# A perceiver block on one core: operands moved to one address phase, retention in halves of 64 tokens, cross-attention scores by head in sixteen tiles of the array

## What is computed

```python
x = x + cross_attention(layernorm(x), ctx, ctx)      # x: 32 items x 32 tokens x 512; ctx: 32 x 257 x 512
#   16 heads of 32: scores = Q K^T / sqrt(32); scores <= thr -> -1e9; softmax; @ V; @ Wo.T + bo
x = x + retention_stack(layernorm(x))                # 2 layers
#   xn = LN(x); q, k rotated; scores = (q k^T) * decay, causal inside an item; out = scores v
#   8 heads of 64; y = groupnorm(out); x = (silu(xn Wg) * y) Wo + x
#   x = gelu(LN(x) W1) W2 + x                         # 512 -> 2048 -> 512
x = x + mixture(layernorm(x))                        # 8 experts 512 -> 1024 -> 512, top 2 of each token
```

## Time and profile before

| | |
|---|---|
| median of 3 runs | 1723.44 us (1722.08 to 1725.44) |
| the profiled execution: its time, its span | 1722.73 us, 1720.9 us |
| mean granted TensorE clock | 0.987 |
| cross-attention, keys of item 0 to the last scores | 43 to 547 us |
| retention, layer 0 and layer 1 | 576 to 721 us, 916 to 1062 us |
| feed-forward, layer 0 and layer 1 | 721 to 911 us, 1062 to 1254 us |
| mixture groups | 1290 to 1710 us |

### The profile page before, as it was taken

The page is one execution under the profiler, slowest core; times in us unless marked ns, Lnnn a source line. Parts: engine busy times, 40 slices in busy tenths (PEclk is TensorE's granted clock), DMA queues, the critical chain, the costliest instruction groups (busy, mean ns, idle before and its releaser), DMA issues.

```text
span 1720.9 us, 29176 instructions
## 1 busy us (share of the span) xinstructions
PE 1649.3 (96%) x10832; PEld 1402.7 (82%) x10832; DVE 1087.0 (63%) x2138; ACT 851.2 (49%) x1195; POOL 471.8 (27%) x357
## 2 busy tenths in 40 slices
PE   7999999999998899999998999999989999999997
PEld 6888889889887688788887887887877888888886
DVE  6554454554556767653337676635457989999995
ACT  4444444344444333344335233534416787878873
POOL 1443443444343344300004443300021121211311
PEclk9999999999999899999999999999999999999999
DMA  5011101110111300023224001224342443626612
GB/s 195 26 38 39 37 24 37 37 37 24 61 49 48 113 1 1 25 86 98 91 93 142 1 1 35 88 88 146 133 163 71 172 159 93 246 74 244 215 48 67
DMA packets 35977, 144.00 MB, mean 84 GB/s; under 512 B 4992, under 2 KB 5504, under 8 KB 28672
## 3 DMA queue, kind: packets, MB, share of 16 engines
q1 hardware_dynamic: 30736, 130.98, 21.7%
q0 software_dynamic: 5168, 12.06, 3.5%
HBM read 222.72 MB, written 12.85 MB: 137 GB/s over the span
## 4 chain that ended last, share of the span: by engine, by line
PE 56%; DVE 6%; DMA 2%; issue 1%; ACT 1%; SPq 0%; POOL 0%; DVEq 0%; POOLq 0%; ACTq 0%
PE bank L88 35%; PE bank L1608 9%; PE bank L2083 7%; PE bank L1505 2%; PE bank L2089 2%; PE bank L1592 1%; DVE e_w L2010 1%; DVE rc L1253 1%; DVE rs L1253 1%; DMA A<-xh_d,token 1%; DMA out<-acc_d 0%; PE bank L1517 0%; PE bank L1627 0%; DVE r_xh L1230 0%; DVE r_wg L1239 0%
## 5 line engine op out<-in xcount | busy, mean ns | idle before, releaser
L2010 DVE TENSOR_TENSOR e_w<-e_raw,e_w 128x2048 fp32r<-128x2048 f32 x134 | 302.4, 2284 | 20.3 <-ACT e_w L1892 19.8
L1892 ACT ACTIVATE e_w<-e_raw 128x2048 fp32r<-128x2048 f32 x134 | 256.6, 1918 | 38.4 <-PE bank L2083 19.2
L88 PE MATMUL bank<-e_w,e_xT 128*128 128x512 f32 x1104 | 272.1, 396 | 0.0
L88 PEld LDWEIGHTS bank<-e_w,e_xT 128*128 128x128 f32 x1104 | 204.3, 188 | 42.5
L88 PE MATMUL bank<-wv,ctx 128*128 128x512 f32 x768 | 190.8, 397 | 6.9 <-DVE kT L669 6.9
L88 PE MATMUL bank<-ctx,wk 128*128 128x258 f32 x1536 | 193.3, 285 | 2.1 <-issue 2.1
L88 PE MATMUL bank<-x2T,fw 128*128 128x512 f32 x768 | 190.4, 398 | 4.7 <-DVE fw L1314 4.7
L88 PEld LDWEIGHTS bank<-ctx,wk 128*128 128x128 f32 x1536 | 186.9, 190 | 4.0 <-issue 2.9
L1608 PE MATMUL bank<-fw,hh 128*128 128x512 f32 x768 | 186.1, 391 | 2.7 <-DVE hh L1432 2.7
L88 PEld LDWEIGHTS bank<-x2T,fw 128*128 128x128 f32 x768 | 145.2, 191 | 35.9 <-issue 5.0
L1608 PEld LDWEIGHTS bank<-fw,hh 128*128 128x128 f32 x768 | 143.9, 188 | 34.6 <-issue 2.2
(11 more groups left out here) (253 smaller groups left out, 2674.4 us busy)
## 6 DMA issues: line engine op xcount, KB each, us to landing
e_raw<-in_we SPq DMA_DIRECT2D x138, 1024.0 KB, 5.6
fraw<-in_wf SPq DMA_DIRECT2D x64, 512.0 KB, 3.5
ctxraw<-in_ctx SPq DMA_DIRECT2D x32, 514.0 KB, 3.5
wraw<-in_wa SPq DMA_DIRECT2D x20, 512.0 KB, 4.4
X<-in_x SPq DMA_DIRECT2D x4, 512.0 KB, 7.0
acc_d<-X SPq DMA_DIRECT2D x8, 256.0 KB, 4.5
xh_d<-A SPq DMA_DIRECT2D x8, 256.0 KB, 3.7
out<-acc_d SPq DMA_DIRECT2D x4, 512.0 KB, 5.9
```

The costliest lines, as they stand in the source:

```text
L88: last = nc.tensor.matmul(out, lhs(t, a), rhs(t, b), start=start and n == 0, stop=n == len(steps) - 1)
L1892: nc.scalar.activation(w[pos][:, 0, :, :], raw[pos][:, :, :], ACT.Copy).then_inc(m["w_hi"], 1)
L2010: nc.vector.tensor_tensor(w[pos][:, 1, :, :], raw[pos][:, :, :], r(w[pos][:, 0, :, :]), ALU.subtract).then_inc(m["w_lo"], 1)
```

## The change

- **Addresses.** A helper `to_line` fills up to the next address that is 64 bytes past a multiple of 512; `X`, the identity, `A`, `wk`, `wv`, `wo`, `oT_hl`, `ctx` and with them `e_hT`, `yT` and `x2T0` start there. A row of `ctx` is 384 elements apart (258 used).
- **Scores by head.** `kT` and the queries are plain float32. POOL copies the 32 queries of an item (`qb`) instead of building `qbd`; PE does 16 float32 matmuls of 32x32 with 257 columns, one to each place of the array (head g of a group in rows 32g, group c in columns 32c), into banks 4, 5, 2, 3. The low parts of q and k (L548, L669 on DVE) are gone. `u`, `pr` and `pT` are indexed by g instead of c; the spread matmul has `plast` stationary and the identity moving.
- **Order in cross-attention.** Values of rows 0 to 127, then all scores, then values of rows 128 to 255; `project` (k = 1) and `turn(b-1)` behind them. `attend` is now of item b-2 and stands between the second and the third chunk of the keys. On DVE `heads(b-2)`, `bias_heads` and `project_lo` come before the thresholds, all four thresholds together, then the terms, `last_token(b-1)`, the products. `add_x` moves from k = 1 to k = 2.
- **Retention in halves.** Scores: two 64x64 matmuls per head, for tokens 0 to 63 and 64 to 127 against themselves, in four tiles of the array. `pf` and `decay` are half as wide. `apply_scores`: two matmuls per head over 64 rows.
- `norm_apply` of the next tile stands before the second `rotate`.

```diff
+def to_line(nc, holder, name):
+    gap = (LINE_AT + -nc.sbuf_base // 32 * 32) % LINE      # LINE, LINE_AT = 512, 64
+    if gap:
+        holder(name, [P, gap // 4])
...
-                    def score(b, cs, begin):
...
-                            products(nc, bank[2 + c % 2][:, 0:SKE], range(1), lambda _, h: qbd[:, h, c, :],
-                                     lambda _, h: kT[:, h, c, :]).then_inc(s_ps, 1)
+                    def score():
+                        for g in range(HPC):
+                            rows = slice(g * XD, (g + 1) * XD)
+                            for c in range(DC):
+                                last = nc.tensor.matmul(bank[S_BANK[g]][c * S:(c + 1) * S, 0:SK], qb[rows, c, :], kT[rows, c, :], start=True, stop=True)
+                        last.then_inc(s_ps, 1)
...
+                                if dc == 1 and not (first and k < 2):
+                                    if not (first and k == 2):
+                                        pe.wait_ge(oT_ok, b - 2)
+                                    attend((k - 2) % BPT, b - 2, it if k == 2 and not first else None)
...
-            last = nc.tensor.matmul(bank[7][:, h * E:(h + 1) * E], pf[:, h % 2, h // 2, :], vv[:, h * E:(h + 1) * E], ...)
+            for two in PAIR:
+                last = nc.tensor.matmul(bank[7][two, h * E:(h + 1) * E], pf[two, h % 2, h // 2, :], vv[two, h * E:(h + 1) * E], ...)
...
-                    last_mm = nc.tensor.matmul(bank[2 + i][:, c * P:(c + 1) * P], kT[rows, c, :], qT[rows, c, :], ...)
+                    for two in PAIR:
+                        last_mm = nc.tensor.matmul(bank[2 + i][two, c * E:(c + 1) * E], kT[rows, c, two], qT[rows, c, two], ...)
...
+                            if not (begin or end):
+                                norm_apply(n + 1, t + 1)
                             rotate(n, 1)
```

More of the change, by code:

```diff
@@ L33 @@
 SKE = SK + 1
+CTX_ROW = 3 * P
 XH = 16
@@ L666, in body @@
                             final = last and k == BPT - 1
-                            for dc in range(DC):
-                                dve.wait_ge(k_hi, DC * b + dc + 1)
-                                nc.vector.scalar_tensor_tensor(kT[:, 1, dc, :], bank[K_BANK[dc]][:, 0:SKE], col("bk", dc), r(kT[:, 0, dc, :]),
-                                                               ALU.add, ALU.subtract).then_inc(k_lo, 1)
-                                if dc == 1 and k == 1 and not first:
-                                    project_lo(it - 1)
+                            if k == 2 and not first:
+                                add_x(it - 1)
+                            if not (first and k < 2):
+                                heads((k - 2) % BPT, b - 2)
                             if k == 1 and not first:
-                                add_x(it - 1)
+                                bias_heads(it - 1)
+                                project_lo(it - 1)
                             if final:
@@ L776, in turn @@
                         pe.wait_ge(plast_ok, b + 1)
-                        nc.tensor.matmul(bank[6][:, 0:P], same_head[:, :], plast[:, :, :].rearrange("p c n -> p (c n)"),
+                        if not (isinstance(b, int) and b == 0):
+                            pe.wait_ge(olast_ok, b)
+                        nc.tensor.matmul(bank[6][:, 0:P], plast[:, :, :].rearrange("p g n -> p (g n)"), ident[:, :],
                                          start=True, stop=True).then_inc(spread_ps, 1)
@@ L815, in body @@
                             pe.wait_ge(ctx_lo, b + 1)
+                            if first and k < 2:
+                                pe.wait_ge(zeroed, k + 1)
                             for dc in range(DC):
@@ L829, in body @@
                             if not begin:
-                                pe.wait_ge(k_lo, DC * b + DC)
                                 turn(b - 1)
-                            score(b, (0, 1), begin)
-                            value(1)
-                            score(b, (2, 3), begin)
-                            if not begin:
-                                if not (first and k == 1):
-                                    pe.wait_ge(oT_ok, b - 1)
-                                attend(k - 1, b - 1, it if k == 1 and not first else None)
                     body(0, True)
@@ L1336, in body @@
                                 dve.wait_ge(m["a0_ok"], NT)
-                            if not (begin or end):
-                                norm_apply(n + 1, t + 1)
                             if begin:
@@ L1516, in apply_scores @@
                         for h in range(H):
-                            last = nc.tensor.matmul(bank[7][:, h * E:(h + 1) * E], pf[:, h % 2, h // 2, :], vv[:, h * E:(h + 1) * E],
-                                                    start=True, stop=True)
+                            for two in PAIR:
+                                last = nc.tensor.matmul(bank[7][two, h * E:(h + 1) * E], pf[two, h % 2, h // 2, :], vv[two, h * E:(h + 1) * E],
+                                                        start=True, stop=True)
                         last.then_inc(m["o_ps"], 1)
```

209 lines of the change are left out of this document (106 added, 103 removed).

## The result

| | before | after |
|---|---|---|
| median of the runs, us | 1723.95 (1722.08 to 1725.44, 4 runs) | 1670.92 (1667.59 to 1674.09, 4 runs) |
| profiled execution, us | 1722.73, span 1720.9 | 1671.40, span 1669.6 |
| PE busy, us | 1649.3 | 1602.9 |

The ratio is 0.9693, 95% interval 0.9671 to 0.9714: 53 us faster. The forecast was 1670, between 1654 and 1694.

The account below looks back on a forecast made before the run. PE's queue of matmuls was taken to bound the kernel (96% busy). Gains of 21 + 14.4 + 18.4 - 1 + 1 = 54 us from 1722.7 gave 1669 profiled, about 1670 us median; range 1656 to 1684, 1654 to 1694 with the first two rivals.

Parts of the forecast that it names:

- Addresses: Operands of PE's matmuls moved to 64 bytes past a multiple of 512: 21 us gained (12 to 23).
- the keys' 7.7 us: Key products of cross-attention: 5 ns a matmul gained from the new places, 0.24 us an item, 7.7 us.
- if the keys stay at 120 ns a matmul: Sign in the profile after: key matmuls of 258 columns unchanged at 120 ns would show the forecast wrong.
- Feed-forward: First halves, 32 `up` and 32 `down` runs of 12 matmuls: 0.05 us each from the new places, 3.2 us.
- Mixture: 46 `e_hT` runs and as many behind them: 0.11 us each pair from the new places, 5.1 us.
- Values: 64 value runs of cross-attention: from 2.78 to 2.73 us each by the new places, 3.2 us.
- The first rival: The new places bring nothing elsewhere; 21 us less gained, 1691 us, chance 0.13.
- Scores: Cross-attention: 16 tiled float32 matmuls at 1.0 us replace 1.45 us an item, 14.4 us gained.
- The third rival: Score matmuls' sixteen places don't run together: two at a time 1750 us, chance 0.05; four 1724, chance 0.03.
- Retention: Halves and earlier `norm_apply`: apply 13.6 us, scores 4.8 us, together 18.4 us gained (3 to 24).
- Waits: Cross-attention on PE: waits for kT and `add_x` go, a 1.4 us wait in seven tiles comes; 1 us lost.
- The end of cross-attention: PE's 5.6 us stand for the last normalisation shortens because its softmax starts earlier; 1 us gained.

Follow-up runs that it names:

- keys_width: Changed kernel with the second and fourth key product of each item widened from 258 to 384 and 320 columns; 1695.81 us.
- addr_old: Changed kernel with operand places as before the change (but wo at 192, oT_hl at 96), the rest as changed; 1678.95 us, ratio 0.9742.

## Why the prediction was right

The time came within 1 us of the forecast, and the main mechanisms held; the terms did not all.

1. **Addresses: 21 forecast, 10 measured.** The step that failed is the keys' 7.7 us. I scaled 227 ns for 512 columns to 114 for 258 and took the rest of the 120 for something that the place could cure. keys_width shows a fixed 13 ns in each matmul, and addr_old gives 1.6 us. The prediction called itself wrong "if the keys stay at 120 ns a matmul", and they did: on that count it was wrong, and the sum held because other terms were better. The other terms, start to start, with the places put back against as changed:
   - Feed-forward: 2 us of 3.2 in its runs. The stages gained 3.6, but one layout's executions differ by as much there (201.0 to 203.3 and 140.7 to 142.4 us).
   - Mixture: 2.9 of 5.1. The `e_hT` runs behind an `e_xT` run gained their 0.08 (2.80 to 2.72), and the 44 `e_xT` runs behind `e_hT` their 0.03 (2.754 to 2.725). I had priced all 46 `e_hT` runs like the first kind; about half stand behind a transpose and gained 0.03. The 46 `e_xT` runs behind a transpose lost 0.6 us in all, and why isn't known.
   - Values: 2.1 of 3.2 (185.0 to 182.9 us for 64 runs). `yT` 0.7 and `oT_hl` 0.8, together 1.5 of 1.9.

   The first rival (worth nothing elsewhere) falls with addr_old.

2. **Scores: 14.4 forecast, 32 x (1.45 - 0.85) = 19.2.** The mechanism was right: sixteen places run together. The group took 0.65 us where 0.6 of stream and 0.13 of tail were forecast, and the slower steps beside it 0.2 where some 0.3 of switching was left. How much of the 0.65 is stream isn't shown, so the split of the forecast's 1.0 is untested. The third rival (two or four at a time) is refuted by 0.65 us against its 2.7 or more.

3. **Retention: 18.4 forecast, 18.5 less 0.7 of `yT`.** The total is right, its parts only partly: apply 1.08 for 1.2, scores 0.63 for 0.8, and the neighbours took 0.1 back. I priced the moved `norm_apply` at the 0.2 us wait it removes. Undone alone it costs 10.1 us, not 3.2: once apply is 1 us shorter, PE comes that much earlier to the same wait.

4. **Waits: -1 forecast.** kT's 6.9 went, 8.0 came (7 of 1.2, forecast 1.4; its own terms, 4.2 - 2.9, give 1.3, and PE comes to `attend` at 3.1). The "about 2 more at `attend` for `add_x`" was misread: the 2.1 us were the gaps in front of the keys at the turn of the loop. They went too, so the sum is +1. Not forecast: the lower clock behind the 2.41 us wait, 1.6 us. One trace of the kernel before shows it, so how often it comes is open.

5. **The end of cross-attention: 1 forecast.** PE's idle time there went from 5.6 + 2.0 (for `xn`) to 2.56 + 1.05 + 1.97 us:
```profile
525.61 1.08 PE L790 MATMUL bank<-pT,v 128*32 128x32 f32 x64 [2.56 <-issue]
527.74 1.97 PE L772 MATMUL bank<-ident,pr 128*128 128x128 f32 x8 [1.05 <-POOL pr L362]
...
533.97 3.02 PE L99 MATMUL bank<-r_wq,xn 128*128 128x512 f32 x12 [1.97 <-DVE xn L713]
```
2 us gained.

Together: 54 forecast; -11 addresses, +5 scores, +2 waits, +1.6 the clock in the first item, +1 end, -0.6 retention, -3.4 the start by chance. That is 49 of the 51.3 of the two spans. Of the rest 1.5 lie in the feed-forward stages and 1.2 between `r_wq` and the first `r_xh`, where executions of the new kernels differ by as much (15.4 to 16.7). The closeness is in part luck: errors that cancelled, 11 us of addresses against 5 of scores, 2 of waits and what the clock gave and took.

## What to carry to other kernels

Before a run is scaled from one width to another, fit its pace from two widths: here a full 128 x 128 matmul is its columns and a fixed part, and nothing tried here shortened the fixed part. When the work ahead of a short wait is made shorter, price the edit that removes the wait together with it: the wait grows as work ahead of it is saved, and the two edits were worth 0.5 and 0.4 us a tile apart but 1.4 together. Before a stage's difference is put down to the change, look for stretches of lower clock in both traces. After such a change read the new wait's chain on the other engine for idle stretches; the 8 us that were left went with one instruction moved into one.

## What the runs showed of the hardware

- The pace of full 128 x 128 products depends on how the stationary and the moving operand lie to each other, counted past a multiple of 512 bytes: for 512 columns 227 ns at a difference of 0 (both at 64, or both at 96), about 230 at 320 (`x2T`), 233 to 235 at 64, 96 and 128. With 258 columns it was 1 ns. The Trainium skill, "SBUF — State Buffer", "SBUF: two separate sides", gives PE two independent read ports, one for each operand; these rows disagree in so far as the places interact.
- A run with both operands at the same place pays too when it stands between displaced ones: `fw,hh` 2.77 us beside `x2T` at 320, 2.76 at 96, 2.73 at 128, and 2.72 beside `x2T` at 0. Why isn't shown.
- A full matmul costs 12.5 to 14 ns over its columns at 2.4 a ns, from 258 to 512 columns alike.
- Sixteen tiles of 32 x 32 all run at once: 32 records of 257 columns, 387 ns each on average by the profile, within 0.65 us, whichever of rows or columns comes first. A second group behind the first costs 0.78.
- A wait of 0.20 us behind the full-tile `apply` run cost 0.36, since PE also loses the overlap of the next instructions with its tail.
- At the start, PE's clock rose before 13.2 us in some executions and after 18.6 us in others of the same start, worth 3 to 4 us of a run, and the granted clock in the rows read 1.00 in both.
- Behind one and the same wait of 1.80 us the clock stayed at 1.00 in one execution and fell to 0.66 in another (1.7 us). Behind the wait of 2.41 us in the kernel before, it was 0.67.
